# Two feed-forwards in token halves, with attention of the other half between their products, on one Trainium2 core

## What is computed

```python
x = x + tanh(g_ffn[1]) * L1_ffn(layernorm(x), ...)          # 32 experts, top 4
x = x + tanh(g_xattn[2]) * L2_xattn(layernorm(x), ctx, Wq, Wk, Wv)
x = x + tanh(g_ffn[2]) * L2_ffn(layernorm(x), ...)
x = x + tanh(g_xattn[3]) * L3_xattn(layernorm(x), ctx, wq, bq, wkv, bkv, wp, bp)
x = x + tanh(g_ffn[3]) * L3_ffn(layernorm(x), ...)

# L2_xattn: 32 heads of 8; q and k divided by their root mean square, softmax(q k' / sqrt(8)) v
# L3_xattn: 16 heads of 16; q = qdq(x) @ qdq(wq).T + bq; out = qdq(o) @ qdq(wp).T + bp
#           qdq: symmetric int8 rounding by the largest magnitude of a token
# L2_ffn: 8 experts of 256 hidden features, all computed; weights from a "golden zone" router
# L3_ffn: 8 experts of 512 hidden features, all computed; top-p router
out_e = (silu(x @ gate[e]) * (x @ up[e])) @ down[e]
out   = sum_e weight[:, e] * out_e
```

## Time and profile before

| | |
|---|---|
| median of 3 runs | 1105.65 us (1105.06 to 1105.92) |
| the profiled execution | 1108.61 us, of which the span from first to last instruction is 1106.8 us |
| busy: PE, DVE, ACT, POOL | 838.1, 674.0, 456.9, 233.5 us |
| granted TensorE clock, mean | 0.853 |

### The profile page before, as it was taken

How to read it: one execution, slowest core, us unless ns; L and a number is a source line. 1 busy time by engine, 2 the same in 40 slices (tenths; PEclk the granted TensorE clock), 3 DMA queues, 4 the chain that set the end, 5 groups by cost and what they waited for, 6 DMA issues and landing times.

```text
span 1106.8 us, 17371 instructions
## 1 busy us (share of the span) xinstructions
PE 838.1 (76%) x6240; PEld 539.3 (49%) x6240; DVE 674.0 (61%) x1366; ACT 456.9 (41%) x850; POOL 233.5 (21%) x247
## 2 busy tenths in 40 slices
PE   4885689995504787304598899992976999999998
PEld 2434446654303566203366456651653555666664
DVE  4968634448752777334554677678876655555554
ACT  2554533442202888302553344432743344444442
POOL 3977223331372000371200000004200000000000
PEclk9776699998656999756696799995876999999999
DMA  9422044431024888330000011110000111111111
GB/s 331 163 71 69 1 123 130 126 87 44 10 100 136 289 273 287 134 100 14 1 17 1 27 46 43 57 43 0 3 2 15 58 43 57 43 57 44 55 43 53
DMA packets 42953, 88.39 MB, mean 80 GB/s; under 512 B 5385, under 2 KB 17033, under 8 KB 42898
## 3 DMA queue, kind: packets, MB, share of 16 engines
q1 hardware_dynamic: 31618, 70.90, 20.1%
q0 software_dynamic: 3072, 8.39, 2.4%
q10 hardware_dynamic: 8208, 8.39, 2.1%
HBM read 64.03 MB, written 23.63 MB: 79 GB/s over the span
## 4 chain that ended last, share of the span: by engine, by line
PE 57%; issue 12%; DVE 12%; POOL 8%; DMA 5%; ACT 5%; SPq 1%; POOLq 0%; ACTq 0%; DVEq 0%
PE ps L1124 28%; PE ps L1140 13%; DMA arena<-seats 2%; POOL arena L653 2%; PE ps L1412 2%; PE ps L1426 2%; PE ps L1234 2%; PE ps L1086 1%; DVE stats L1593 1%; POOL k_st L570 1%; PE ps L1219 1%; POOL k_st L565 1%; DMA ctx_sb<-in_ctx 1%; PE ps L1440 1%; POOL arena L543 1%
## 5 line engine op out<-in xcount | busy, mean ns | idle before, releaser
L1124 PE MATMUL ps<-turned_buf,W 128*128 128x512 f16 x1512 | 357.2, 388 | 8.4 <-DVE W L1751 5.9
L1124 PEld LDWEIGHTS ps<-turned_buf,W 128*128 128x128 f16 x1512 | 150.4, 100 | 171.1 <-issue 18.1
L1140 PE MATMUL ps<-W,arena 128*128 128x256 f16 x1512 | 186.3, 274 | 9.7 <-DVE arena L1746 9.7
L1140 PEld LDWEIGHTS ps<-W,arena 128*128 128x128 f16 x1512 | 148.4, 98 | 53.3 <-issue 8.3
L1739 DVE SCALAR_TENSOR_TENSOR arena<-ps,arena 128x512 f32<-128x512 f32 x126 | 86.9, 689 | 116.4 <-ACT arena L838 116.0
L1746 DVE TENSOR_TENSOR arena<-arena 128x512 f16<-128x512 f32 x126 | 87.6, 695 | 97.4 <-ACT arena L864 92.5
L838 ACT ACTIVATE arena<-ps 128x512 f32<-128x512 f32 x126 | 74.9, 595 | 165.2 <-PE ps L1124 164.7
L864 ACT ACTIVATE arena<-arena 128x512 f16<-128x512 f32 x126 | 79.4, 630 | 135.0 <-DVE arena L1739 70.9
L1086 PE MATMUL ps<-ident,xn 128*128 128x128 f32 x112 | 24.7, 404 | 79.6 <-DVE xn L1617 79.6
L525 POOL TENSOR_TENSOR rstd<-veps,mhalf 128x4 f32<-128x4 f32 x16 | 17.9, 1118 | 286.1 <-DVE veps L1598 286.1
L1086 PEld LDWEIGHTS ps<-ident,xn 128*128 128x128 f32 x112 | 20.9, 211 | 82.9 <-DVE xn L1617 79.1
(11 more groups left out here) (328 smaller groups left out, 1288.6 us busy)
## 6 DMA issues: line engine op xcount, KB each, us to landing
W<-in_w SPq DMA_DIRECT2D x79, 384.0 KB, 3.1
seats<-wq ACTq DMA_DIRECT2D x1, 8192.0 KB, 36.9
arena<-seats SPq DMA_DIRECT2D x32, 256.0 KB, 3.5
served<-arena SPq DMA_DIRECT2D x32, 256.0 KB, 2.1
wb<-in_w SPq DMA_DIRECT2D x16, 384.0 KB, 3.4
wb<-routed SPq DMA_DIRECT2D x16, 256.0 KB, 3.8
folded<-W SPq DMA_DIRECT2D x4, 384.0 KB, 2.3
W<-folded SPq DMA_DIRECT2D x4, 384.0 KB, 3.2
```

What stands on the lines that cost most here:

```text
L1124: last = nc.tensor.matmul(bank(2 * g + half), W16[:, k % 2, w, g * D + c * P:g * D + (c + 1) * P], x16[:, i, c, half * HALF:(half + 1) * H ...
L1140: last = nc.tensor.matmul(ps[:, 4 + t // 2, (t % 2) * D:(t % 2 + 1) * D], f_h16[:, k % 2, i, t * S:(t + 1) * S], W16[:, k % 2, w, 2 * D:3 ...
```

## The change

Feed-forward 2 and feed-forward 3 each become two passes, one per token half (`PASS`: pass 0 and 1 are layer 2, half 0 and 1; pass 2 and 3 are layer 3). A pass uses four PSUM banks, 4 (gate), 5 (up), 6 and 7 (output); banks 0 to 3 are left to attention. A pass is a list of steps: an even step makes gate and up of tile k, an odd one the down products of tile k - 1. The other half's attention is written between the steps, in the same order on all engines:

- half 0 of attention 2 is normalised, transposed and multiplied while half 1 is still being gathered; the loop has 64 units of 4 heads (exponentials of 512 elements), the work that prepares half 1 stands at units 2 to 23, and from unit 50 (`FIRST_UNIT`) each unit takes one step of pass 0; the rest of pass 0 holds the end of half 1;
- pass 1 and pass 2 are each spread over 44 slots (`LATE`) that hold attention 3 of half 0 and of half 1 at the slots of `MAX_AT` and so on; `steps_by` says how many steps have run by a slot. Pass 3 is alone. Both kinds of scores of attention 3 share banks 0 and 1, and the maxima are kept per block, not per unit;
- the weights are split once per layer, in passes 0 and 2: high part on ScalarE, low part on GpSimd in two instructions (in pass 2 every second tile on VectorE in one). SP writes each split tile to DRAM (`keep`) and passes 1 and 3 read it back (`again`) into four slots `w4`;
- router weights are computed per half (`l_w`); the adds of an expert are `half_add`, four instructions; from unit 37 the copies of attention 2's outputs, and all those of attention 3, are ScalarE's; the copies of q into two parts are one instruction with a repeated input.

The core of the diff (by engine: setup, SP, GpSimd, ScalarE, TensorE, VectorE, and TensorE's slots; those of the other engines follow the same list):

```diff
+        kept = [None, None] + [nc.dram_tensor(f"kept_{L}", (NT[L], P, 2 * WROW), F16, kind="Internal").ap() for L in (2, 3)]
...
+        w4 = [W16[:, 0, :, :], W16[:, 1, :, :]] + \
+            [wb16[:, 2 * WROW * k:2 * WROW * (k + 1)].rearrange("p (i d) -> p i d", i=2) for k in range(2)]
...
+        PASS = ((2, 0), (2, 1), (3, 0), (3, 1))
+        PASS_AT = (0, NT2, 2 * NT2, 2 * NT2 + NT3)
+        SPLIT_AT = (0, None, NT2, None)
+        KEPT_AT = (0, 0, NT2 // 4, NT2 // 4)
+        EXPERTS_AT = (0, E2, 2 * E2, 2 * E2 + E3)
+        FIRST_UNIT = 50
+        LATE = 44
+        MAX_AT = (15, 16, 17, 18, 21, 22, 25, 26)
+        NM_AT = (17, 19, 23, 27)
+        LESS_AT = (19, 20, 23, 24, 27, 28, 29, 30)
+        WEIGH_AT = (20, 21, 24, 25, 28, 29, 30, 31)
+        O_AT = (22, 26, 30, 32)
+
+        def steps_by(h, s):
+
+            if h == 1:
+                return min((s + 1) * 7 // 5, 2 * NT3)
+            if s < 14:
+                return s + 1
+            return min(14 + (s - 13) * 11 // 19, 25) if s < 33 else min(25 + s - 32, 2 * NT2 + 2)
+
+        def by_dve(p, k):
+
+            return p == 2 and k % 2 == 1
...
+            def fresh(n):
+
+                sp.wait_ge(sem("wgu_lo"), tiles(2) + n - 1)
+                sp.dma_start(W[:, n % 2, :], source(2, n) if n < NT2 else source(3, n - NT2)).then_inc(sem("w_in", n % 2), 16)
+
+            def keep(p, k):
+
+                sp.wait_ge(sem("wgu_lo"), tiles(2) + SPLIT_AT[p] + k + 1)
+                sp.dma_start(kept[PASS[p][0]][k].rearrange("p (i d) -> p i d", i=2), w4[k % 4]).then_inc(sem("kept", k % 4), 16)
+
+            def again(p, k):
+
+                sp.wait_ge(sem("kept", k % 4), 16 * (KEPT_AT[p] + k // 4 + 1))
+                sp.wait_ge(sem("down_done"), tiles(2) + PASS_AT[p] + k - 3)
+                sp.dma_start(w4[k % 4], kept[PASS[p][0]][k].rearrange("p (i d) -> p i d", i=2)).then_inc(sem("slot_in", k % 4), 16)
...
+            for p in (0, 2):
+                n = NT[PASS[p][0]]
+                for k in range(n):
+                    if SPLIT_AT[p] + k + 2 < NT2 + NT3:
+                        fresh(SPLIT_AT[p] + k + 2)
+                    keep(p, k)
+                for k in range(n):
+                    again(p + 1, k)
...
+            def split_lo(p, k):
+
+                n = SPLIT_AT[p] + k
+                pool.wait_ge(sem("wgu_hi"), tiles(2) + n + 1)
+                link(nc.gpsimd.tensor_scalar(W[:, n % 2, :], W[:, n % 2, :], WSCALE, None, ALU.mult))
+                if p:
+                    pool.wait_ge(sem("wgu_lo"), tiles(2) + n)
+                nc.gpsimd.tensor_tensor(w4[k % 4][:, 1, :], W[:, n % 2, :], w4[k % 4][:, 0, :], ALU.subtract)                    .then_inc(sem("wgu_lo"), 1)
+
+            def half_step(p, st):
+
+                k = st // 2
+                if st % 2 and p % 2 == 0 and k + 2 < NT[PASS[p][0]] and not by_dve(p, k + 2):
+                    split_lo(p, k + 2)
...
+            def half_silu(p, k):
+
+                g = PASS_AT[p] + k
+                act.wait_ge(sem("gate_mm"), g + 1)
+                if g >= 2:
+                    act.wait_ge(sem("gated"), HALVES + g - 1)
+                nc.scalar.activation(h_s[:, g % 2, :], bank(4), ACT.Silu, scale=1.0 / WSCALE).then_inc(sem("silu_done"), 1)
+
+            def half_hi(p, k):
+
+                g = PASS_AT[p] + k
+                act.wait_ge(sem("gated"), HALVES + g + 1)
+                if g >= 2:
+                    act.wait_ge(sem("down_done"), tiles(2) + g - 1)
+                nc.scalar.activation(h_16[:, g % 2, 0, :], h_g[:, g % 2, :], ACT.Copy).then_inc(sem("h_hi"), 1)
+
+            def split_hi(p, k):
+
+                n = SPLIT_AT[p] + k
+                act.wait_ge(sem("w_in", n % 2), 16 * (slot_tiles(2, n % 2) + n // 2 + 1))
+                if p or k >= 4:
+                    act.wait_ge(sem("down_done"), tiles(2) + PASS_AT[p] + k - 3)
+                else:
+                    act.wait_ge(sem("e_down"), E1)
+                if k >= 4:
+                    act.wait_ge(sem("kept", k % 4), 16 * (KEPT_AT[p] + k // 4))
+                nc.scalar.activation(w4[k % 4][:, 0, :], W[:, n % 2, :], ACT.Copy, scale=WSCALE).then_inc(sem("wgu_hi"), 1)
+
+            def half_step(p, st):
+
+                k, n = st // 2, NT[PASS[p][0]]
+                if st % 2 == 0 and k < n:
+                    half_silu(p, k)
+                if st % 2 and k < n:
+                    half_hi(p, k)
+                    if p % 2 == 0 and k + 2 < n:
+                        split_hi(p, k + 2)
...
+            q2_x(0)
+            q2_square(0)
+            q2_guess(0)
+            q2_hi(0)
+            for n in range(8 * B + 2):
+                if n == 12:
+                    q2_x(1)
+                if n == 16:
+                    q2_square(1)
+                if n == 19:
+                    q2_guess(1)
+                if n == 23:
+                    q2_hi(1)
+                if n in (40, 42):
+                    split_hi(0, n // 2 - 20)
+                if n == 47:
+                    half_x(5, 0)
+                if n >= FIRST_UNIT:
+                    half_step(0, n - FIRST_UNIT)
+                if n == 50:
+                    golden_sigmoid(0)
+                if n == 52:
+                    golden_exp(0)
+                if n >= 37 and n % 4 == 1:
+                    o2T(n // 4 - 1)
+                if n < 8 * B:
+                    p2_exp(n)
...
+            def half_gate_up(p, k):
+
+                g, half = PASS_AT[p] + k, PASS[p][1]
+                if p % 2 == 0:
+                    pe.wait_ge(sem("wgu_lo"), tiles(2) + SPLIT_AT[p] + k + 1)
+                else:
+                    pe.wait_ge(sem("slot_in", k % 4), 16 * (E1 // 4 + KEPT_AT[p] + k // 4 + 1))
+                for n, read, done in ((0, "silu_done", "gate_mm"), (1, "gated", "gu_done")):
+                    if g:
+                        pe.wait_ge(sem(read), HALVES + g)
+                    for c in range(KD):
+                        for i, w in THREE:
+                            last = nc.tensor.matmul(bank(4 + n), w4[k % 4][:, w, n * D + c * P:n * D + (c + 1) * P],
+                                                    x16[:, i, c, half * HALF:(half + 1) * HALF],
+                                                    start=(c == 0 and i + w == 0), stop=(c == KD - 1 and w == 1))
+                    last.then_inc(sem(done), 1)
+
+            def half_down(p, k):
+
+                g, per = PASS_AT[p] + k, G[PASS[p][0]]
+                first, final = k % per == 0, k % per == per - 1
+                pe.wait_ge(sem("h_lo"), HALVES + g + 1)
+                if first and g:
+                    pe.wait_ge(sem("out_read"), EXPERTS_AT[p] + k // per)
+                elif first:
+                    pe.wait_ge(sem("golden"), 1)
+                for t in range(4):
+                    for w, i in THREE:
+                        last = nc.tensor.matmul(ps[:, 6 + t // 2, (t % 2) * D:(t % 2 + 1) * D],
+                                                h_16[:, g % 2, i, t * S:(t + 1) * S], w4[k % 4][:, w, 2 * D:3 * D],
+                                                start=(first and t % 2 == 0 and i + w == 0), stop=final,
+                                                skip_group_check=True)
+                last.then_inc(sem("down_done"), 1)
+
+            def half_step(p, st):
+
+                k, n = st // 2, NT[PASS[p][0]]
+                if st % 2 == 0 and k < n:
+                    half_gate_up(p, k)
+                if st % 2 and k:
+                    half_down(p, k - 1)
+                if st == 1 and p % 2:
+                    half_down(p - 1, n - 1)
...
+            for t in range(4):
+                add_back(t)
+            statistics(4, 0)
+            add_back(4)
+            normalise(4, 0)
+            add_back(5)
+            q2_squares(0)
+            q2_norm(0)
...
+                if n in (2, 4):
+                    add_back(5 + n // 2)
+                if n == 5:
+                    statistics(4, 1)
+                if n == 8:
+                    normalise(4, 1)
+                if n == 18:
+                    q2_squares(1)
+                if n == 22:
+                    q2_norm(1)
...
+            def half_gated(p, k):
+
+                g = PASS_AT[p] + k
+                dve.wait_ge(sem("silu_done"), HALVES + g + 1)
+                dve.wait_ge(sem("gu_done"), HALVES + g + 1)
+                if g >= 2:
+                    dve.wait_ge(sem("h_lo"), HALVES + g - 1)
+                nc.vector.scalar_tensor_tensor(h_g[:, g % 2, :], bank(5), 1.0 / WSCALE, h_s[:, g % 2, :],
+                                               ALU.mult, ALU.mult).then_inc(sem("gated"), 1)
+
+            def half_lo(p, k):
+
+                g = PASS_AT[p] + k
+                dve.wait_ge(sem("h_hi"), HALVES + g + 1)
+                nc.vector.tensor_tensor(h_16[:, g % 2, 1, :], h_g[:, g % 2, :], h_16[:, g % 2, 0, :], ALU.subtract)\
+                    .then_inc(sem("h_lo"), 1)
```

(60 more changed lines are left out.)

1014 lines of the change are left out of this document (563 added, 451 removed).

## The result

| | before | after |
|---|---|---|
| median (lowest to highest), 7 runs each | 1105.88 us (1104.05 to 1112.26) | 1117.15 us (1111.26 to 1120.73) |
| the profiled run; its span | 1108.61 us; 1106.8 us | 1111.26 us; 1109.4 us |
| TensorE busy, share of the span | 838 us, 76% | 861.1 us, 78% |
| mean granted clock of the profiled run | 0.853 | 0.870 |

After over before is 1.0092, with a 95% interval of 1.0062 to 1.0122. The kernel became **slower by 0.9%**; the forecast was 1081 us, 2.2% faster. A second series on another occasion gave 1118.10 us and 1.0121 (1.0082 to 1.0161). A few executions in later series took 1265 to 4590 us and are left out of every ratio.

The account below looks back on a forecast made before the run. TensorE's idle and half-clock time outside the feed-forwards was taken as the time to win. 584 + 91 + 115 + 157 + 128 + 7 = 1082 us of span, less 1.2, gave 1081 us; range 1035 to 1122.

Parts of the forecast that it names:

- Attention 2 starts earlier: First scores of attention 2: half 0 goes ahead alone, so the loop starts at 511.4 instead of 538.84, 27 us earlier.
- The loop up to unit 50: Attention 2 loop to the first feed-forward product: 50 us of units plus 22.7 put in, 72.7 us, ending at 584.
- 8.0 each: Attention 2 loop: time per batch row before, against 6.4 us at full clock, since part ran at 1.2 GHz.
- The bound of 90: Attention 2 loop: upper bound in us, if nothing put in is hidden and 12 copies each add a wait of 0.69 + 0.2.
- Pass 0: Half 0 of feed-forward 2: 77.7 us of TensorE work, +6 for ScalarE, +7 for expert-weight blocks, 91 us.
- 5.15 against 5.21, so it just fits: Weight split on GpSimd: loop through it 5.15 us against TensorE's 5.21 in between, so it adds nothing at a 2.9 us split.
- Pass 1: Half 1 of feed-forward 2 with attention 3 of half 0: 86.4 us of TensorE work, +15, +8, +4, +1, 115 us.
- Pass 2: Half 0 of feed-forward 3 with attention 3 of half 1: 149 us, +8 for VectorE blocks, 157 us.
- A: Rival: waits outside the feed-forwards are filled nearly everywhere; 1030 to 1060 us, chance 0.24.
- B: Rival: idle gaps in passes 0 to 2 drop the clock to 1.2 GHz for feed-forward tiles; 1140 us, chance 0.16.
- C: Rival: ScalarE's function-table changes lie on the path, adding 20 + 9 us; 1109 us, chance 0.08.
- D: Rival: attention 3 does not overlap the feed-forwards, only the earlier start remains; about 1095 to 1105 us, chance 0.08.

Follow-up runs that it names:

- e15: Changed kernel with scores in pairs, preparation spread, GpSimd's split multiply left out and a plain copy for Silu (result not computed): 1076.39 us, 0.9765.
- e2: Changed kernel without GpSimd's multiply in its weight splits (result not computed): 1107.39 us, ratio to before 1.0018.
- e3: Changed kernel with a plain scaled copy for Silu in the last two feed-forwards (result not computed): 1103.70 us, ratio to before 0.9969.
- e4: Changed kernel with the preparation of the second half's queries spread over units 22 to 30: 1113.46 us, ratio to before 1.0125.
- e5: Changed kernel with 38 unread products of 512 columns added ahead of the scores of units 20 to 25: 1114.62 us, ratio to before 1.0107.
- e7: Changed kernel with scores of units 16 to 43 of attention 2 in pairs on two row groups and two banks: 1110.26 us, ratio to before 1.0055.
- e6: Changed kernel with low parts of the splits of passes 0 and 2 on VectorE, but for three tiles: 1116.35 us, ratio to before 1.0083.
- e13: Changed kernel with the Silu of passes 0 to 2 written by Tanh plus one more VectorE instruction a tile: 1118.52 us, ratio to before 1.0104.
- e10: Changed kernel with scores of units 16 to 43 in pairs, preparation spread and all splits but three on VectorE: 1101.76 us, ratio to before 0.9960.
- e8: Changed kernel with scores of units 16 to 43 in pairs and the second half's preparation spread: 1105.27 us, ratio to before 1.0013.
- e1: Kernel before with the eight score products of an attention 2 unit reordered, four to one row group, then four to the other: 1113.08 us, ratio 1.0093.
- e0_before: Kernel before, unchanged, run again against itself: ratio 1.0015 (0.9988 to 1.0042).

## Why the prediction was wrong, step by step

**Attention 2 starts earlier: right.** 511.4 forecast (the steps as written add up to 511.9), 509.3 and 513.8 measured, against 538.84.

**The loop up to unit 50: wrong, 72.7 against 87.3 and 91.9.** The step that failed is "with the same products in total". The count is the same; but a unit of four heads has its scores on one row group, so they cost 0.39 us for four heads instead of 0.40 for eight, and as much again at the lower clock. By the groups of both traces, TensorE's score products went from 14.6 to 31.8 us busy, part of it by the clock. The second part is the gap of 5.2 us, which was in the sum (8.6 us for refinement and splitting), though not as a stop of the exponentials. The third is the clock: I let "8.0 each" of before stand for the share at 1.2 GHz, and it became 41 us in one run and 54 (the gap among them) in the other; what holds it down there stays open. With pairs and the preparation spread, the loop is 75.5 to 78 us; with e15's lighter engines 72.8. The bound of 90 does not come out of its terms either: 50 + 22.7 + 12 x 0.89 is 83.4, below both profiles.

**Pass 0: 91 against 93.9.** The estimate of the loop through the split, "5.15 against 5.21, so it just fits", rested on 0.9 us for GpSimd's one-input multiply. It takes 2.17, above my upper end of 1.8. With the subtract at 1.64 (under the 1.8 to 2.8 of the earlier trace rows) the split is 3.8 us instead of 2.9, which cost 7.8 us here (e2). That the pass came within 2.9 us of its forecast is luck: I had charged 6 us for the table loads of its first seven tiles, and taking all loads away gave 0.7 (e3).

**Pass 1: 115 against 116.0, pass 3 and the end: 135 against 133.6.** Both hold, pass 1 partly by luck: the table loads that I had put at nothing there cost 4 us, and other waits were that much smaller.

**Pass 2: 157 against 169.3.** Two terms at nothing: the split (8.4 us by e2; my text had 14 at its upper end) and the tables (8.8 by e3). With both away it is 156.2.

**The profiled run.** I set the median 1.2 us under the span. After's profiled run is the fastest of its seven: the median lies 7.8 us above its span. That is 9 us of the 36; the stages are the other 27 (14.6 + 2.9 + 1.0 + 12.3, less 2.1 and 1.4).

**The rivals.** A (1030 to 1060) is out. B named the right engine state and the wrong place: passes 0 to 2 run at 0.95 to 0.98, and the low clock is in the attention loop, where I had written that "today this hits only attention products"; its lead from an idle gap to a long low clock is what e4 and e5 refute. C is right in kind: 14 us for the tables; its price of 28 us was too high. So was the one with the drain, for which the sum is 1100 rather than 1099. D is out, the passes do overlap. None of the cases had two moderate misses together, which is what happened, and the range ended at 1122 only because of B.

## What to carry to other kernels

Before halving a unit of small products, look at which row groups of the array it leaves: four products on one group cost what eight on two cost, and two spare banks for every second pair of units gave back 7.8 us (e7). Where an estimate says "it just fits", the term in it with no row of its own decides; here it was wrong by 1.3 us and cost 10. And a repair that moves work to the engine with the most free time is to be costed in that engine's fixed order: the multiply and the tables together were worth 22 us when left out, and each only 0 to 4 when moved to VectorE (e6, e13, and e10 against e8).

## What the hardware showed that I had not expected

- Products on two row groups, writing two banks, run beside each other even when four in a row come for one group: eight in 0.40 and 0.41 us in the two orders (before, e1), four on one group in 0.39. On one group they start 56 ns apart at 2.4 GHz and 107 at 1.2.
- In attention 2 the granted clock was 0.50 for 40 us and more with TensorE busy for 94 to 96% (after, e4, e5), whether or not an idle gap came first. In the loop of one and the same kernel a low stretch that began at 575 to 580 was over at 585 in one profile (e0_before) and at 593 in another (before).
- The time of a run goes with its mean clock: lines through the runs of before give 0.7 to 0.9 us for each 0.001 (in e1's series 1099 us at 0.863, 1115 at 0.846), and a reordering that left every unit's duration as it was moved both (e1).
- GpSimd's multiply by a constant, 128x768 f32 in place, takes 2.17 us on the mean; its two-input subtract of the same size with an f16 output 1.64 at the median; VectorE does both in one instruction of 0.95.
- 384 KB written to DRAM land in 4.2 us and are back in 3.0; with 48 such writes and as many read-backs TensorE waited for one of them once, 1.9 us.
